# Attention products: both query halves of a key tile issued as one run on TensorE

## What is computed

```
scores = jnp.einsum('bhqd,bhkd->bhqk', Q, K) / np.sqrt(D_HEAD)
causal = jnp.triu(jnp.full((t, t), -jnp.inf, dtype=scores.dtype), k=1)
attn = jax.nn.softmax(scores + causal, axis=-1)
O = jnp.einsum('bhqk,bhkd->bhqd', attn, V)
```

## Time and profile before

| | |
|---|---|
| Median of 3 runs | 3473.13 us |
| Profiled execution | 3477.08 us |
| Its span | 3475.4 us |
| TensorE busy | 3238.5 us (93%) |
| VectorE busy | 2632.0 us (76%) |
| ScalarE busy | 1736.9 us (50%) |
| GpSimd busy | 1130.8 us (33%) |

### The profile page before, as it was taken

How to read it: one execution, slowest core, us unless ns; L and a number is a source line. 1 busy time by engine, 2 the same in 40 slices (tenths; PEclk the granted TensorE clock), 3 DMA queues, 4 the chain that set the end, 5 groups by cost and what they waited for, 6 DMA issues and landing times. The chain is left out here.

```text
span 3475.4 us, 68174 instructions
## 1 busy us (share of the span) xinstructions
PE 3238.5 (93%) x22540; PEld 1965.8 (57%) x22540; DVE 2632.0 (76%) x5407; ACT 1736.9 (50%) x3363; POOL 1130.8 (33%) x1888
## 2 busy tenths in 40 slices
PE   4979999999999979999997977999999979999999
PEld 2643444444444347777774544555556546777776
DVE  6538888888888759999995995555565548999997
ACT  3644666666666633333333653555555543333333
POOL 2452222222222222222223664444444442222222
PEclk9998999999999989999998998999999989999999
DMA  4764333333333122222223655444444522222221
GB/s 116 236 204 90 84 83 84 84 84 84 83 84 84 36 74 88 83 88 84 88 71 109 207 194 127 105 113 111 102 106 106 113 61 83 83 88 84 88 84 55
DMA packets 390580, 350.25 MB, mean 101 GB/s; under 512 B 111814, under 2 KB 331846, under 8 KB 390214
## 3 DMA queue, kind: packets, MB, share of 16 engines
q1 hardware_dynamic: 390342, 347.10, 37.5%
HBM read 210.12 MB, written 135.27 MB: 99 GB/s over the span
## 5 line engine op out<-in xcount | busy, mean ns | idle before, releaser
L814 DVE TENSOR_REDUCE aA_nmax<-bank 128x1 f32<-128x512 f32 (+3 forms) x1216 | 715.8, 656 | 166.7 <-PE bank L872 88.1
L853 ACT ACTIVATE aA_prob<-bank 128x512 f32<-128x512 f32 (+1 forms) x1216 | 605.4, 586 | 292.9 <-PE bank L898 292.0
L1211 DVE TENSOR_REDUCE aB_nmax<-bank 128x2 f32<-128x512 f32 (+1 forms) x512 | 324.9, 657 | 207.6 <-PE bank L1305 200.4
L872 PE MATMUL bank<-aA_ks,aA_qs 96*128 96x512 bf16 (+3 forms) x1536 | 447.3, 335 | 36.8 <-DMA aA_ks<-parts_A 20.5
L898 PE MATMUL bank<-aA_qs,aA_ks 99*128 99x512 bf16 (+3 forms) x1536 | 406.0, 330 | 6.2 <-DMA aA_qs<-aA_rows 4.5
L1274 ACT ACTIVATE aB_prob<-bank 128x512 f32<-128x512 f32 (+1 forms) x512 | 271.6, 571 | 135.4 <-PE bank L1305 131.3
L917 PE MATMUL bank<-aA_prob,aA_vq 128*32 128x512 f32 (+3 forms) x3072 | 316.7, 507 | 0.0
L797 POOL TENSOR_TENSOR aA_spare<-aA_spare 128x1 f32<-128x1 f32 x256 | 49.7, 194 | 762.4 <-ACT aA_prob L853 762.4
L1305 PE MATMUL bank<-aB_ks,aB_qs 96*128 96x256 bf16 (+3 forms) x2048 | 245.5, 258 | 30.4 <-DMA aB_own<-own_d 28.4
L872 PEld LDWEIGHTS bank<-aA_ks,aA_qs 96*128 96x128 bf16 x1536 | 148.8, 98 | 204.5 <-DVE aA_nmax L814 121.8
L898 PEld LDWEIGHTS bank<-aA_qs,aA_ks 99*128 99x128 bf16 x1536 | 124.6, 97 | 233.7 <-ACT aA_prob L853 145.3
(11 more groups left out here) (242 smaller groups left out, 6596.6 us busy)
## 6 DMA issues: line engine op xcount, KB each, us to landing
parts_A<-pA_part SPq DMA_DIRECT2D x96, 256.0 KB, 3.3
aA_qs<-parts_A SPq DMA_DIRECT2D x192, 128.0 KB, 3.9
aA_ks<-parts_A SPq DMA_DIRECT2D x192, 128.0 KB, 4.0
parts_B<-pB_part SPq DMA_DIRECT2D x96, 256.0 KB, 2.6
aB_qs<-parts_B SPq DMA_DIRECT2D x192, 128.0 KB, 3.9
aB_ks<-parts_B SPq DMA_DIRECT2D x192, 128.0 KB, 4.1
o_A<-aA_o_sb SPq DMA_DIRECT2D x32, 512.0 KB, 3.1
o_B<-aB_o_sb SPq DMA_DIRECT2D x32, 512.0 KB, 3.1
```

The lines of the kernel that those rows point to most:

```text
L814: nc.vector.tensor_reduce(dst, src, AX.X, ALU.max, negate=True).then_inc(s["max_taken"], 1)
L853: nc.scalar.activation(dst, src, ACT.Exp, scale=SCALE).then_inc(s["exp_done"], 1)
L872: ins = nc.tensor.matmul(out, qs[g][0:KROWS, h, q * P:(q + 1) * P], ks[g][0:KROWS, h, k0:k0 + kw], start=True, stop=True, skip_group_check ...
L1211: nc.vector.tensor_reduce(dst, src, AX.X, ALU.max, negate=True).then_inc(s["max_taken"], 1)
```

## The change

The p units of a key tile are no longer two elements of the list for tiles 0 to 3 but one, whose cost in the planner is that of all its columns. It may be placed once the last exp unit of the tile's *second* half is done. When TensorE comes to it, it issues both halves one after the other. The matmuls themselves, their waits and their operands are the same. The same diff changes what `weave` returns for everything else.

```diff
@@ -660,9 +660,8 @@ def dense_order():
-    for (k, c), i in sorted(LAST_EXP.items()):
-        cols = (c + 1) * 4 * P - max(k * P, c * 4 * P)
-        pvs.append((("pv", k, c), 1.67 * cols + 20, [("exp", i)], None, 0))
+    for k in range(QT):
+        pvs.append((("pv", k, 1), 1.67 * (T - k * P) + 40, [("exp", LAST_EXP[k, 1])], None, 0))
     return weave([exps, maxs, pvs], {"rows": 3000}, 220, 300)
@@ -930,7 +929,8 @@ def group(b, g, more):
                         if kind == "exp":
                             exp_unit(b, g, i)
                         elif kind == "pv":
-                            pv(b, g, i, *half)
+                            for c in range(i // 4, 2):
+                                pv(b, g, i, c)
```

## The result

| | before | after |
|---|---|---|
| Median | 3473.39 us | 3622.91 us |
| Lowest to highest of 4 runs | 3470.93 to 3473.67 | 3622.28 to 3623.07 |
| Profiled execution, span | 3477.08, 3475.4 us | 3622.78, 3621.1 us |

The changed kernel is slower: ratio 1.0432, 95% interval 1.0414 to 1.045, 149.5 us. The forecast was 3643 us (170 us slower).

The account below looks back on a forecast made before the run. TensorE bounds the kernel (93% busy). Period 5.12 + 8.4 + 9.9 + 8.5 + 1.8 = 33.7 us for 29.35; 136 us over 31 periods plus 34 for the clock makes 170, so 3643 us, range 3570 to 3685.

Parts of the forecast that it names:

- Places of runs: Isolated p runs on TensorE stand in 8 places instead of 9; one place saved, 0.28 us a period.
- From t0 to e0: Turn to first exp unit: 5.12 us instead of 5.38, TensorE waiting for the rows, without p4 to p7 to fill it.
- From e0 to p0: First exp unit to first run: 7.1 us of TensorE work and 1.3 of waits, 8.4 in all.
- From p0 to t0: First run to next turn: runs 9.9, exp and max units 8.5, waits 1.8 us (p4 0.65, p5 0.3, turn 0.8).
- The clock: TensorE at half clock after e0 in most groups: 1.1 us a period, 34 us in all, between 0 and 65.
- waits alone: Rival: the waits come as walked but TensorE's clock holds, 3609 us; chance 0.30.
- the signs named ahead: Turns 33 to 35.5 us apart, e0 5.0 to 5.2 after, p4 wait 0.65, clock under 1.00, VectorE about 70%.
- the main loss: p4 to p7 no longer filling the gap behind the turn: 2.13 - 0.26 = 1.9 us a period.

Follow-up runs that it names:

- experiment 4: Kernel before with the halves of p0 to p3 joined at their second halves, turn still ahead of p4 to p7: 3472.48 us, ratio 1.0000.
- experiment 7: Kernel before, halves not joined, with m0 to m2 of the next list issued between the turn and p4: 3469.04 us, ratio 0.9987.
- Experiments 7 and 8: The second of these is experiment 7 with the last exp unit moved to the end of the list, behind the turn: 3456.38 us, ratio 0.9953.
- experiment 3: Changed kernel with eight unneeded matmuls per group behind m2 to m5, between turn and e0: 3582.26 us, ratio 1.0318.
- Experiment 2: Kernel before with the turn moved behind p7 and eight unneeded matmuls per group behind m2 to m5: 3525.32 us, ratio 1.0152.
- exp. 6: The kernel of experiment 5 with unneeded matmuls behind its last three max units, ahead of the turn: 3547.38 us, ratio 1.0201.
- experiment 5: Changed kernel with its last exp and max units reordered so the turn stands ahead of p4 to p7: 3573.34 us, ratio 1.0288.
- experiment 1: Kernel before with only the turn moved, behind p7; no run joined: 3573.6 us, ratio 1.0291.

## Why the prediction was right

The direction, the places and most sizes came out as walked. By the steps:

- **Places of runs.** The list has one place fewer, and experiment 4 shows that even four fewer change nothing measurable. As TensorE's time the price of a place stands: both halves of p0 together take 1.88 us, eight blocks at 0.213 and the fixed 0.18 once. In the period four such savings were without worth. In my walk one place is 9 of 170 us.
- **From t0 to e0.** Predicted 5.12, measured 4.60 to 4.64 in 26 of 31 groups. This term was mis-sized: I took the journey of the last group before, 5.05, and did not ask why VectorE's last row step took 0.74 us. In that period GpSimd cleared the last diagonal at the same moment, 729.24 to 729.87. The new list has it done before the turn. Experiments 7 and 8 show it with one unit swapped. The trace of the kernel before had the answer too: at its first turn, 285.56, GpSimd has nothing to do, the step took 0.28 us, and e0 came 4.75 us after the turn, at half clock. Worth 0.5 x 31, 15 us less loss. Timelines of VectorE and TensorE, kernel before:

```profile
286.85 0.28 DVE L833 TENSOR_TENSOR aA_rows<-aA_left,aA_rows 32x128 bf16<-32x128 f32 x1
...
290.31 1.46 PE L898 MATMUL bank<-aA_qs,aA_ks 99*128 99x512 bf16 x3 [0.72 <-DMA aA_qs<-aA_rows]
```

- **From e0 to p0.** Predicted 8.4 at full clock; 8.21 in experiment 3.
- **From p0 to t0.** Predicted 20.2 with 1.8 of waits; measured 19.87 (711.48 to 731.35). The waits in it, less the 0.10 that stands before any run: p4 0.5 (predicted 0.65), p5 0.2 (0.3), t0 0.76 (0.8).
- **The clock.** Predicted 34 us, most groups; measured 41 (3622.9 - 3582.3), by experiment 3, and it fell in each of the 30 periods behind the first. The mechanism was worked out from rows, the size was not: 1.1 us a period was a choice between 0.7 and 2.1, and that it came so near 1.4 is in part luck. Experiment 2 shows the same without joined runs, 48 us. The rival "waits alone", 3609, is out: its kernel is experiment 3, and it stands at 3582 because the journey is shorter. The Trainium skill's table ("TensorE: Matmul & The Clock Gate", section "Why this matters for your kernels") names idle gaps between bursts. The traces do not agree that such a gap is needed: at 699.2 above the clock fell with matmuls in the gap and no idle over 0.7 us.

Of the signs named ahead, the turns are 33.7 to 34.7 us apart, VectorE is busy for 23.86 of 34.34 us (69%), the clock is under 1.00, and p4 waits for GpSimd; only e0 stands closer to the turn than I said.

The sum: 170 - 15 (journey) - 6 (head) - 10 (tail) + 7 (clock) = 146; measured 149.5 by the medians and 145.7 in the profiled executions. The terms that missed were too large by 31 us and too small by 7, so a part of the misses cancelled.

At full clock four lists form a square, and each corner was run:

| period at full clock, us | turn before p4 to p7 | turn last |
|---|---|---|
| units woven | 29.35 (before) | 31.03 (exp. 2) |
| units bunched, runs joined | 31.64 (exp. 6) | 32.71 (exp. 3) |

The turn's place costs 1.7 alone and 1.1 beside the bunching; the bunching costs 2.3 alone and 1.7 beside the turn. In times of kernels, by the ratios: turn 53 us (1.0152), bunching 58 more (to 1.0318), clock 40 more. The other way round it is bunching 70 (1.0201), turn 41, clock 40. So at full clock the bunching weighs more than the turn's place by either way, and "the main loss", as I called the 1.9 us of the turn, was wrong. My own sum said so: of its 4.35 us a period only 1.9 were the turn's.

Why together they cost less than the two sides added (3.4 against 4.0) was not tried by a run, but the traces show where it sits. With the turn last the stretch from p0 to the turn grows by 2.4 us in the woven list (20.00 to 22.41) and by only 1.8 in the bunched one (18.07 to 19.87). In the bunched list TensorE waits 1.64 us for VectorE just before the early turn (experiment 5) and 0.70 before the late one (the changed kernel), where p5 to p7 are issued meanwhile. The square is also not clean in its lower row: the list of experiment 6 has its last units woven by hand, and p4 to p7 in one place and not four.

The loss comes from the planner's new list and not from the joined runs as such: experiment 4 joins the same runs, keeps the rest of the list and loses nothing. Whether the new list would lose less with its halves apart was not tried. Nor was it tried that the planner placed the turn last because it counts 3.0 us from the turn to the rows, where 4.6 to 5.1 pass.

## What to carry to other kernels

When an edit goes through a planner, compare the two lists before counting what the edit saves: here it said "8 instead of 12" and meant 8 instead of 9 places, and it moved the start of a 5 us round trip through three engines behind the work that hid it. Find each such trip, time it where nothing covers it, and see what each list issues during it. Then ask what TensorE does in the hole, since the hole can cost a second time through the clock: eight matmuls that nobody needs made this kernel 41 us faster.

## What the runs showed of the hardware

- A VectorE step with two inputs from SBUF (32x128, L833) takes 0.28 us alone and 0.74 us when GpSimd's clearing of 128x512 runs beside it; started 0.03 us after GpSimd's instruction of 0.63, it ended 0.14 after it (726.22 and 726.25, experiment 7). In the joined list of experiment 4 it started 0.24 after GpSimd's instruction of 0.70, took 0.60, and again ended 0.14 after it. In these traces the step's end follows the end of GpSimd's instruction. This agrees with the Trainium skill ("SBUF — State Buffer", section "Who interferes with whom"), which says that such an instruction contends with a GpSimd instruction that reads SBUF, and that the later one is held until the first is done. VectorE's reductions out of PSUM did not stretch: in the kernel before, those of 512 columns took 0.68 us in the median, beside a clearing and without one.
- TensorE's clock fell with matmuls running: in the changed kernel 699.2, with TensorE at work on m0 to m2 until 698.5 and on m3 from 699.13; in experiment 5 at 743.7, during p4 to p7, after three max units 0.6 us apart and 1.64 us of idle before the turn. Matmuls that nobody needs, put into these gaps, kept it at 1.00 in all 30 periods behind the first in three lists (experiments 2, 3 and 6). It cost 1.4 us of a 34 us period in the changed kernel and up to 3.1 (34.1 against 31.0) in experiment 1.
